# A mixture-of-experts stage whose indirect transfers each wait for an assigned tile of TensorE

## The chip, the core and the metric

The kernel runs on one core of one Trainium2 chip. The metric is the time of one execution on the device in microseconds; shorter is better. The kernel before takes 2303.66 us, the median of three runs that lie between 2303.51 and 2306.36 us.

The engines are named as the profile names them: PE (TensorE, matmuls; PEld is its weight load), DVE (VectorE), ACT (ScalarE), POOL (GpSimd), SP (SyncE, which only issues transfers here).

## The reference, cut to what matters

A batch of 16 sequences of 512 tokens with 128 features goes through two transformer layers. The change lies in the last stage, a mixture of experts that runs twice over all tokens:

```python
for _ in range(LOOPS):                     # 2
    z_norm = _rmsnorm(z, norm_w)
    scores = softmax(z_norm @ router_w)    # 8 experts
    topk_vals, topk_idx = top_k(scores, 2)
    ...                                    # weights of the two chosen, made to sum to 1
    mixed = sum over e of cw[:, e] * _swiglu(z_norm, w1[e], w3[e], w2[e])
    z = z + mixed
```

Each of the 8192 tokens needs only its two chosen experts. So the kernel sorts token rows by expert, runs matmuls on tiles of 128 rows that all belong to one expert, and brings the results back to the tokens.

## The kernel before, in words

`two_layers` runs the attention and feed-forward stages (`middle`, up to about 1500 us of the profile) and then `experts` (from line 1131 on), which the change touches.

**Groups, units, tiles.** A group is 8 blocks of 128 tokens; there are 8 groups, and two rounds (loops), so groups k = 0 to 15 are routed. The sorted rows are worked off in units: unit 0 holds group 0, units 1 to 7 two groups each, unit 8 one. A unit of one group has 23 tiles, one of two groups 39; in all N = 319 tiles, and `base_of` = 0, 23, 62, 101, 140, 179, 218, 257, 296 are the units' first tiles.

**One tile.** SP loads 128 sorted rows from `rows_in` (L1357), up to 8 tiles ahead, after waiting for `step_done` of the tile 7 before it; PE transposes them (L1407, one matmul instruction a tile, which makes it a good counter of tiles), multiplies by w1 and w3 of the expert (L1395), transposes the hidden rows (L1388) and multiplies by w2 (L1402), in a software pipeline that is 8 steps deep (LAG). ACT and DVE move and combine the results; ACT stores 128 rows to `rows_out` (L1465). PE raises the semaphore `step_done` by one at each step, up to N + LAG = 327.

**Side work.** Between the tiles the same engines do the routing of group k in 20 small stages (`side`), spread over 14 or 20 steps from `begin[k]` on. Groups 0 and 1 are done ahead of tile 0. The last stage, 19, writes the rows' addresses (`scat_idx`, L1695) and raises `scat_ready`. Stages 0 to 3 of a group k of 8 or more first add what the gather brought; their DVE instructions wait for that gather and sit in front of the tiles' own.

**Transfers of POOL.** POOL issues nothing here but indirect transfers of 128 rows of 512 bytes. A scatter `s<k>` (L1506) is 16 of them, tokens of group k to their sorted places; a gather `g<k>` (L1519) is 16 that bring the results of group k - 8 back. Each run of 16 is called a burst below. The order is written out by hand in `transfers`:

```python
transfers = ("s0 s1 s2 s3 g8 s4 s5 g9 s6 g10 s7 g11 s8 g12 s9 g13 s10 g14 s11 s12 g15 s13 g16 s14 g17 g18 s15 "
             "g19 g20 g21 g22 g23").split()
```

A scatter waits for the group's rows and for `scat_ready`. A gather waits until all tiles of its unit are stored, and from g11 on for the additions of the gather three before it, whose buffer it takes. Within a burst there are no waits. SP waits before a unit's first load for all scatters of that unit, so a late scatter holds the tile with which the unit begins.

Of the kernel before, what the change touches and what calls it, by code (L numbers as in the profile page):

```python
# [1170 lines left out]
def experts(nc, x, z, w, tri, ins, out, rows_in):  # L1171


    IT = 8
    GROUPS = BATCHES * TILES // IT
    CHUNKS = 4
    SIDES = (LOOPS + 1) * GROUPS
    RING, HELD = 8, 8
    TURN, MULT, LAG = 6, 2, 8
    BANKS = 3  # L1180
    STAGES = 20
# [4 lines left out]
    base_of = [sum(tiles_in[:u]) for u in range(UNITS + 1)]  # L1186
    N = base_of[UNITS]
# [6 lines left out]
    unit_of = [max(u for u in range(UNITS) if first_of[u] <= k) for k in range(LOOPS * GROUPS)]  # L1194
    EARLY = 2
    begin = {2: 0, 3: 14, 4: 29, 5: 47, 6: 63, 7: 78, 8: 95, 9: 115, 10: 135, 11: 157, 12: 179, 13: 201, 14: 223, 15: 246,
             16: 270, 17: 283, 18: 292, 19: 314, 20: 325}
    transfers = ("s0 s1 s2 s3 g8 s4 s5 g9 s6 g10 s7 g11 s8 g12 s9 g13 s10 g14 s11 s12 g15 s13 g16 s14 g17 g18 s15 "
                 "g19 g20 g21 g22 g23").split()

    def length(k):

        return 14 if k < GROUPS else 20 if k < LOOPS * GROUPS else 8
# [13 lines left out]
    def unit_at(n):  # L1217

        return max(u for u in range(UNITS) if base_of[u] <= n)

    def stored_by(u, s):

        return 16 * sum(1 for n in range(base_of[u + 1]) if n % RING == s)

    with ExitStack() as ctx:
        def sb(name, shape, dt):
            return ctx.enter_context(nc.sbuf_tensor("moe_" + name, shape, dt))

        def sem(name):
            return ctx.enter_context(nc.semaphore("moe_" + name))  # L1230
# [37 lines left out]
        lg, sh, sh2, pr, key, at = (  # L1268
            sb(name, [P, IT, EXPERTS], F32) for name in ("lg", "sh", "sh2", "pr", "key", "at"))
# [33 lines left out]
        step_done, x_copied = sem("step_done"), sem("x_copied")  # L1303
# [15 lines left out]
        def tiles_of(k):  # L1319

            return IT * (k % GROUPS)
# [20 lines left out]
        @block.sync  # L1342
        def _(sp):
            sp.dma_start(w13[:, :, 0:FF], ins["L1_ffn_w1"].rearrange("e d f -> d e f")).then_inc(w_in, 16)
            sp.dma_start(w13[:, :, FF:2 * FF], ins["L1_ffn_w3"].rearrange("e d f -> d e f")).then_inc(w_in, 16)
            for e in range(EXPERTS):
                sp.dma_start(w2[:, e, :, :], ins["L1_ffn_w2"][e].rearrange("(c f) d -> f c d", f=P)).then_inc(w_in, 16)
            for n in range(N):
                u = unit_at(n)
                if n == base_of[u]:  # L1350
                    sp.wait_ge(tables, u + 1)
                    for k in range(first_of[u], first_of[u] + sizes[u]):
                        sp.wait_ge(scattered[k % 3], 16 * 2 * IT * (k // 3 + 1))
                row = sp.value_load(row_of[0:1, n:n + 1], min_val=0, max_val=EXPERTS * CAP - P)
                if n >= RING:
                    sp.wait_ge(step_done, n - RING + 1)
                sp.dma_start(xin[:, n % RING, :], rows_in[u % CHUNKS][bass.ds(row, P), :]).then_inc(x_loaded[n % RING], 16)  # L1357
# [131 lines left out]
        @block.gpsimd  # L1489
        def _(pool):  # L1490
            pool.iota(iota_i[:, :], [[1, MOST]], base=0, channel_multiplier=0)
            pool.iota(reg_i[:, :], [[CAP, EXPERTS]], base=0, channel_multiplier=0)
            pool.iota(fall_i[:, :], [[-1, EXPERTS]], base=EXPERTS, channel_multiplier=0)
            pool.memset(upper[:, :], 1.0)
            pool.memset(ones[:, :], 1.0).then_inc(const, 1)
            pool.wait_ge(const, 1)
            pool.affine_select(out=upper[:, :], in_=upper[:, :], compare_op=ALU.is_gt, fill=0.0, base=0,
                               pattern=[[1, P]], channel_multiplier=-1).then_inc(const, 1)

            def scatter(k):  # L1500
                loop, t0, u = k // GROUPS, tiles_of(k), unit_of[k]
                pool.wait_ge(xn_ready, k + 1)
                pool.wait_ge(scat_ready, k + 1)
                for a in range(2):
                    for t in range(IT):
                        pool.indirect_dma_start(rows_in[u % CHUNKS],  # L1506
                                                bass.IndirectOffsetOnAxis(ap=scat_idx[:, loop, a, t0 + t:t0 + t + 1], axis=0),
                                                xn[:, k % 3, t, :], None).then_inc(scattered[k % 3], 16)

            def gather(k):  # L1510
                loop, t0, u = k // GROUPS - 1, tiles_of(k), unit_of[k - GROUPS]
                pool.wait_ge(tables, u + 1)
                for s in range(RING):
                    pool.wait_ge(y_stored[s], stored_by(u, s))
                if k >= GROUPS + 3:
                    pool.wait_ge(added, k - GROUPS - 2)
                for a in range(2):
                    for t in range(IT):
                        pool.indirect_dma_start(yg[:, k % 3, a, t, :], None, rows_out[u],  # L1519
                                                bass.IndirectOffsetOnAxis(ap=gat_idx[:, loop, a, t0 + t:t0 + t + 1], axis=0))\  # L1520
                            .then_inc(gathered[k % 3], 16)

            for name in transfers:
                if name[0] == "s":
                    scatter(int(name[1:]))
                else:
                    gather(int(name[1:]))

        @block.vector
        def _(dve):  # L1530
# [221 lines left out]
def two_layers(nc, ins, out):  # L1752
    with ExitStack() as ctx:
# [57 lines left out]

        z = sb("z", [P, BATCHES * TILES, DIM], F32)
        experts(nc, x, z, w, tri, ins, out.rearrange(rows, p=P), rows_in)


# [22 lines left out]
```

## Time and profile before

| | before |
|---|---|
| median of the timed runs | 2303.66 us (2303.51 to 2306.36) |
| the profiled execution, its span | 2763.4 us |
| up to the experts stage, in the profile | about 1500 us, then about 100 us without tiles |
| first and last tile transposed | 1599.98 us and 2701.29 us |
| PE, DVE, ACT, POOL busy, share of the span | 76%, 67%, 53%, 44% |
| mean granted TensorE clock | 0.886 of full speed |

The execution that was profiled has a span of 2763.4 us; it is 460 us, or 20%, longer than the median of the timed ones. The page gives no time for it beside the span. A busy time is that of one engine; its share is taken over stages with different limits, so it has to be read stage by stage. "Issue" and "remote" are names for a wait whose end the trace doesn't explain by an instruction of this core's engines.

### The profile page before, as it was taken

The page shows a single profiled execution, that of the slowest core. Times are in us where ns is not written, and L with a number is a line of the kernel's source. Part 1 is how long each engine was busy: PE and PEld are TensorE (multiplying, and loading weights), DVE is VectorE, ACT ScalarE, POOL GpSimd, SP SyncE. Part 2 cuts the span into 40 slices and gives each one's busy share as a digit, 9 for nine tenths or more (in the row PEclk, how much of TensorE's full clock was granted, in tenths as well). Part 3 has the DMA queues.
Part 4 walks back from the last instruction along what each step waited for, and adds up shares of the span by engine and source line. Part 5 has one row for each costly group of instructions (what it writes and reads, how often), then busy time and mean ns, then how long its engine had stood idle before and what let it go on. Part 6 is the DMA issues. An engine that isn't in the chain of part 4 may idle for free. (4 is left out here: it accounts for less than half of the span.)

```text
span 2763.4 us, 47500 instructions
## 1 busy us (share of the span) xinstructions
PE 2109.4 (76%) x14679; PEld 1039.5 (38%) x14679; DVE 1847.5 (67%) x5421; ACT 1458.9 (53%) x3354; POOL 1221.4 (44%) x1710
## 2 busy tenths in 40 slices
PE   5999999999899899999999464665747585556662
PEld 1222222222256444444444243443535353344441
DVE  8999999999767788888888453544434344344324
ACT  1888888888833477777777222332314232233231
POOL 5433434332102577777775344244443524443434
PEclk9999999999999899999999677887859677777876
DMA  6535444354101133333332122221212222222322
GB/s 161 138 99 142 116 124 131 101 147 116 40 1 46 48 94 94 89 76 72 94 94 49 57 61 65 60 69 59 76 56 74 67 66 64 65 68 62 88 75 82
DMA packets 224611, 226.95 MB, mean 82 GB/s; under 512 B 34032, under 2 KB 187504, under 8 KB 224368
## 3 DMA queue, kind: packets, MB, share of 16 engines
q1 hardware_dynamic: 152432, 164.62, 22.4%
q0 software_dynamic: 16384, 33.59, 4.1%
q10 hardware_dynamic: 55552, 25.71, 3.2%
q8 instruction: 127, 2.08, 0.3%
q14 instruction: 116, 0.95, 0.1%
HBM read 96.48 MB, written 125.76 MB: 80 GB/s over the span
## 5 line engine op out<-in xcount | busy, mean ns | idle before, releaser
L702 ACT ACTIVATE mid_PT<-mid_ps 128x512 f32<-128x512 f32 (+2 forms) x1792 | 913.6, 568 | 257.7 <-PE mid_ps L583 249.8
L785 DVE TENSOR_REDUCE mid_nmax<-mid_ps 128x1 f32<-128x512 f32 (+2 forms) x1280 | 776.2, 657 | 61.8 <-PE mid_ps L562 36.7
L562 PE MATMUL mid_ps<-KT,QT 48*128 48x512 bf16 (+3 forms) x2048 | 604.6, 351 | 68.3 <-DVE mid_nmax L785 49.7
L1395 PE MATMUL moe_ps<-moe_w,moe_xinT 128*128 x638 | 393.0, 702 | 315.6 <-issue 171.2
L583 PE MATMUL mid_ps<-QT,KT 64*128 64x512 bf16 (+3 forms) x2048 | 562.0, 346 | 2.6 <-ACT mid_PT L702 2.2
L1547 DVE TENSOR_TENSOR moe_h<-moe_ps,moe_sg 128x256 f32<-128x256 f32 x319 | 134.7, 422 | 518.4 <-ACT moe_sg L1459 279.9
L599 PE MATMUL mid_ps<-mid_PT,vv 128*32 128x512 f32 (+3 forms) x4096 | 464.5, 526 | 15.8 <-POOL mid_PT L914 12.0
L1450 ACT ACTIVATE moe_xinT<-moe_ps,norm_w 128x128 f32<-128x128 f32 x319 | 116.8, 366 | 677.4 <-remote 318.3
L1506 POOL DMA_INDIRECT rows_in<-moe_xn,moe_scat_idx x256 | 246.7, 964 | 462.0 <-DVE moe_scat_idx L1695 388.0
L562 PEld LDWEIGHTS mid_ps<-KT,QT 48*128 48x128 bf16 x2048 | 158.9, 94 | 585.5 <-DVE mid_nmax L785 397.6
L1519 POOL DMA_INDIRECT moe_yg<-rows_out,moe_gat_idx x256 | 245.1, 957 | 249.1 <-issue 122.1
L782 DVE CUSTOM_DVE_ANT_0 mid_PT<-mid_ps,mask 128x512 bf16<-128x512 f32 (+1 forms) x512 | 304.3, 619 | 68.6 <-PE mid_ps L562 63.7
L1402 PEld LDWEIGHTS moe_ps<-moe_w,moe_hT 128*128 128x128 f32 x1276 | 221.2, 217 | 198.1 <-issue 198.1
L1395 PEld LDWEIGHTS moe_ps<-moe_w,moe_xinT 128*128 128x128 f32 x638 | 112.5, 221 | 330.8 <-issue 330.4
L1402 PE MATMUL moe_ps<-moe_w,moe_hT 128*128 x1276 | 220.0, 301 | 12.5 <-issue 6.6
L914 POOL TENSOR_SCALAR_AFFINE_SELECT mid_PT<-mid_PT 128x512 f32<-128x512 f32 x256 | 154.8, 635 | 143.7 <-ACT mid_PT L702 142.3
L1388 PE MATMUL moe_ps<-ident,moe_h 128*128 128x128 f32 x638 | 139.6, 304 | 57.9 <-DVE moe_y L1556 41.5
L898 POOL TENSOR_TENSOR x<-x,mid_ao 128x256 f32<-128x256 f32 x32 | 23.2, 725 | 308.4 <-DVE mid_ao L801 308.4
L583 PEld LDWEIGHTS mid_ps<-QT,KT 64*128 64x128 bf16 x2048 | 136.0, 94 | 18.6 <-ACT mid_PT L702 14.9
L599 PEld LDWEIGHTS mid_ps<-mid_PT,vv 128*32 128x32 f32 x4096 | 81.5, 108 | 131.9 <-issue 96.0
L1454 ACT ACTIVATE moe_hT<-moe_ps 128x256 f32<-128x256 f32 x319 | 120.6, 378 | 15.5 <-remote 14.5
L1459 ACT ACTIVATE moe_sg<-moe_ps 128x256 f32<-128x256 f32 x319 | 123.7, 388 | 0.2
(265 smaller groups left out, 3025.7 us busy)
## 6 DMA issues: line engine op xcount, KB each, us to landing
l_spread<-mid_slots SPq DMA_DIRECT2D x128, 384.0 KB, 5.5
rows_in<-mid_blank SPq DMA_DIRECT2D x64, 512.0 KB, 4.3
QT<-l_spread SPq DMA_DIRECT2D x128, 192.0 KB, 4.3
KT<-l_spread SPq DMA_DIRECT2D x128, 192.0 KB, 5.2
moe_xin<-rows_in SPq DMA_DIRECT2D x319, 64.0 KB
rows_out<-moe_y ACTq DMA_DIRECT2D x319, 64.0 KB
x<-in_L_attn_x_dram SPq DMA_DIRECT2D x8, 512.0 KB, 6.6
QT<-mid_mrows SPq DMA_DIRECT2D x256, 6.0 KB
```

The lines of the kernel that those rows point to most:

```text
L562: mm = pe.matmul(ps[:, bank, n_keys * a:n_keys * (a + 1)], QT[rows, par, pair, i * P:(i + 1) * P], KT[rows, par, pair, 0:n_keys], start=Tr ...
L583: mm = pe.matmul(ps[:, bank, m * a:m * (a + 1)], KT[rows, own, pair, i * P:(i + 1) * P], QT[rows, own, pair, SEQ - m:SEQ], start=True, sto ...
L599: mm = pe.matmul(ps[32 * j:32 * j + 32, O, first(kt):SEQ], vv[:, ((r - 3) // 4) % 2, kt, 4 * ((r - 3) % 4) + j, :], weights_of(r - 3, kt, ...
L702: act.activation(weights_of(r, i, heads), ps[:, ring(S2, n - 2, k), 0:widths[i] * len(heads)], ACT.Exp, scale=scale).then_inc(exp_done, 1)
L782: dve.tensor_tensor_reduce(thrown[:, (SLOTS * n + k) % len(S1), 0:width(i)], of, w["mask"][:, SEQ - width(i):SEQ], -1.0, 3.0e38, ALU.add, ...
L785: dve.tensor_reduce(to, of, X_AXIS, ALU.max, negate=True).then_inc(s1_used, 1)
L914: pool.affine_select(out=diagonal, in_=diagonal, compare_op=ALU.is_ge, fill=0.0, base=0, pattern=[[0, 4], [1, P]], channel_multiplier=-1). ...
L1388: mm = pe.transpose(ps[:, bank, H + c * P:H + (c + 1) * P], h[:, v % 4, c * P:(c + 1) * P], w["ident"][:, :])
L1395: mm = pe.matmul(ps[:, GU[v % BANKS], :], xinT[:, v % 2, :], w13[:, bass.ds(expert(v), 1), :].rearrange("p a f -> p (a f)"), start=True, s ...
L1402: mm = pe.matmul(ps[:, bank, Y:Y + DIM], hT[:, v % 2, c * P:(c + 1) * P], w2[:, bass.ds(e, 1), c, :].rearrange("p a d -> p (a d)"), start= ...
L1506: pool.indirect_dma_start(rows_in[u % CHUNKS], bass.IndirectOffsetOnAxis(ap=scat_idx[:, loop, a, t0 + t:t0 + t + 1], axis=0), xn[:, k % 3, ...
L1519: pool.indirect_dma_start(yg[:, k % 3, a, t, :], None, rows_out[u], bass.IndirectOffsetOnAxis(ap=gat_idx[:, loop, a, t0 + t:t0 + t + 1], a ...
```

## The change

A new function `assigned` makes a list of 512 step numbers, one for each indirect transfer in the order of `transfers`. It starts from the step at which the burst can be ready (`ready`), lets the numbers grow by at least a half from transfer to transfer, so that no more than two have the same one, and then walks back so that no number is above that of the step at which the rows are needed (`due_at`). Before each indirect transfer POOL then waits until `step_done` has reached its number; numbers of zero or below give no wait. Nothing is removed or reordered; the waits ahead of a burst stay.

```diff
+    def assigned():
+
+        ready, due_at = [], []
+        for name in transfers:
+            k = int(name[1:])
+            if name[0] == "s":
+                ready += [0 if k < EARLY else begin[k] + 19 * length(k) // STAGES + 1] * (2 * IT)
+                due_at += [base_of[unit_of[k]] - RING] * (2 * IT)
+            else:
+                ready += [base_of[unit_of[k - GROUPS] + 1] + LAG + 1] * (2 * IT)
+                due_at += [begin.get(k, N + LAG + 1) - 1] * (2 * IT)
+        at, spread = -1.0, []
+        for r in ready:
+            at = max(r, at + 0.5)
+            spread.append(int(at))
+        latest = N + LAG
+        for i in range(len(spread) - 1, -1, -1):
+            latest = min(latest, due_at[i])
+            spread[i] = min(spread[i], latest)
+        return spread
...
+            def after_tile(tiles):
+
+                at = next(tiles)
+                if at > 0:
+                    pool.wait_ge(step_done, at)
...
                 for a in range(2):
                     for t in range(IT):
+                        after_tile(tiles)
                         pool.indirect_dma_start(rows_in[u % CHUNKS],
...
+            tiles = iter(assigned())
```

The same `after_tile(tiles)` stands before the indirect transfer of `gather`. Worked out, the list begins so: s0 gets no wait (its numbers are -8), s1 gets 8, 8, 9, 9 up to 15, 15, s2 gets 15 sixteen times, s3 28 to 35, g8 36 to 43, s4 44 to 51, s5 61 to 68, g9 71 to 78, s6 79 to 86, g10 87 to 94; and it ends with g21 305 to 312, g22 313 to 320 and g23 327 sixteen times.

## Rows read from the trace of the kernel before

**Rows 1.** Page: the span.

```profile
span 2763.4 us, 47500 instructions
```

**Rows 2.** Windows: length; busy us by engine (instructions), granted clock, DMA share, GB/s.

```profile
100.00:1400.00 1300.00, 1200.40 (x9652) 468.72 (x9650) 1134.69 (x2656) 968.10 (x1997) 592.42 (x972) 0.99 0.35 91
...
1600.00:1700.00 100.00, 69.58 (x332) 45.58 (x328) 60.83 (x284) 36.05 (x101) 39.31 (x41) 0.84 0.22 67
1700.00:2700.00 1000.00, 615.93 (x2953) 425.49 (x2954) 402.57 (x1705) 306.31 (x927) 404.67 (x423) 0.77 0.23 67
```

**Rows 3.** Windows of L1407 (one a tile; PE, then PEld): all, burst g13, undisturbed.

```profile
1700.00:2700.00 1000.00, 84.55 (x284) 44.92 (x284) 0.77 0.23 67
2129.50:2149.50 20.00, 1.09 (x4) 0.57 (x4) 0.76 0.28 74
2342.00:2370.00 28.00, 4.09 (x15) 2.15 (x15) 1.00 0.24 68
```

**Rows 4.** Timeline, PE, in the burst g13: start, length, instruction [idle before <-releaser].

```profile
2128.23 0.27 PE L1407 MATMUL moe_ps<-ident,moe_xin 128*128 128x128 f32 x1
...
2129.87 0.27 PE L1407 MATMUL moe_ps<-ident,moe_xin 128*128 128x128 f32 x1
...
2135.74 0.27 PE L1407 MATMUL moe_ps<-ident,moe_xin 128*128 128x128 f32 x1
...
2148.53 2.07 PE L1395 MATMUL moe_ps<-moe_w,moe_xinT 128*128 x2 [12.30 <-issue]
```

**Rows 5.** Waits, whole span: engine, line, what ended them: us, times, longest.

```profile
ACT moe_xinT L1450 <- remote: 318.3, 35, 22.9
```

**Rows 6.** Source lines of scatter (L1506) and gather (L1519): duration ns min/median/max.

```profile
L1506 POOL DMA_INDIRECT rows_in<-moe_xn,moe_scat_idx x256: 952/958/1202, 1573.2 to 2567.9; - x128
...
L1519 POOL DMA_INDIRECT moe_yg<-rows_out,moe_gat_idx x256: 938/944/1939, 1709.0 to 2751.5; - x128
```

**Rows 7.** Timeline, POOL: first and last of s1, first of s2.

```profile
1604.58 0.96 POOL L1506 DMA_INDIRECT rows_in<-moe_xn,moe_scat_idx  x1 [11.18 <-DVE moe_scat_idx L1695]
...
1623.51 0.96 POOL L1506 DMA_INDIRECT rows_in<-moe_xn,moe_scat_idx  x1 [0.30 <-issue]
1643.25 0.96 POOL L1506 DMA_INDIRECT rows_in<-moe_xn,moe_scat_idx  x1 [18.78 <-DVE moe_scat_idx L1695]
```

**Rows 8.** Timeline, POOL: last of s3, then first of g8.

```profile
1707.70 0.96 POOL L1506 DMA_INDIRECT rows_in<-moe_xn,moe_scat_idx  x1 [0.31 <-issue]
1708.96 0.98 POOL L1519 DMA_INDIRECT moe_yg<-rows_out,moe_gat_idx  x1 [0.30 <-issue]
```

**Rows 9.** Windows, all instructions: inside s1 with DVE at work, inside g13 with DVE idle.

```profile
1605.00:1610.00 5.00, 1.94 (x6) 0.58 (x4) 4.52 (x25) 1.54 (x6) 3.78 (x5) 1.00 0.30 90
2140.00:2144.00 4.00, 0.00 (x0) 0.00 (x0) 0.00 (x0) 0.00 (x0) 3.09 (x4) 0.50 0.21 58
```

**Rows 10.** Timeline, POOL, inside g13.

```profile
2142.00 0.94 POOL L1519 DMA_INDIRECT moe_yg<-rows_out,moe_gat_idx  x1 [0.30 <-issue]
2143.24 0.94 POOL L1519 DMA_INDIRECT moe_yg<-rows_out,moe_gat_idx  x1 [0.30 <-issue]
```

**Rows 11.** Timeline, PE and DVE, around s1: tiles' transposes, a chain of small DVE steps.

```profile
1615.90 0.27 PE L1407 MATMUL moe_ps<-ident,moe_xin 128*128 128x128 f32 x1
...
1624.93 0.42 PE L1407 MATMUL moe_ps<-ident,moe_xin 128*128 128x128 f32 x1
...
1603.62 0.17 DVE L1695 CAST moe_scat_idx<-moe_keep_at 128x16 int32<-128x16 f32 x1
...
1615.34 0.17 DVE L92 SCALAR_TENSOR_TENSOR moe_rstd<-moe_rtmp,moe_rstd 128x8 f32<-128x8 f32 x1 [1.22 <-DVE moe_rtmp L91]
```

**Rows 12.** Source L1516 of POOL: waits that stand as instructions of their own.

```profile
L1516 POOLq EVENT_SEMAPHORE  x13: 43/43/43, 1986.3 to 2729.9; - x13
```

**Rows 13.** Timeline, end: POOL's last transfer, DVE after it.

```profile
2751.54 0.94 POOL L1519 DMA_INDIRECT moe_yg<-rows_out,moe_gat_idx  x1 [0.30 <-issue]
2754.09 4.42 DVE L1568 SCALAR_TENSOR_TENSOR z<-moe_yg,moe_keep_w,z 128x128 f32<-128x128 f32 x16 [12.41 <-DMA moe_yg<-rows_out,moe_gat_idx]
```

More of the change, by code:

```diff
@@ L1498, in _, with scatter @@
                                pattern=[[1, P]], channel_multiplier=-1).then_inc(const, 1)
-            def scatter(k):
+            def after_tile(tiles):
+                at = next(tiles)
+                if at > 0:
+                    pool.wait_ge(step_done, at)
+            def scatter(k, tiles):
                 loop, t0, u = k // GROUPS, tiles_of(k), unit_of[k]
@@ L1508, in scatter, with gather @@
                                                 xn[:, k % 3, t, :], None).then_inc(scattered[k % 3], 16)
-            def gather(k):
+            def gather(k, tiles):
                 loop, t0, u = k // GROUPS - 1, tiles_of(k), unit_of[k - GROUPS]
@@ L1518, in gather @@
                     for t in range(IT):
+                        after_tile(tiles)
                         pool.indirect_dma_start(yg[:, k % 3, a, t, :], None, rows_out[u],
@@ L1521, in gather @@
                             .then_inc(gathered[k % 3], 16)
+            tiles = iter(assigned())
             for name in transfers:
                 if name[0] == "s":
-                    scatter(int(name[1:]))
+                    scatter(int(name[1:]), tiles)
                 else:
-                    gather(int(name[1:]))
+                    gather(int(name[1:]), tiles)
         @block.vector
```

## The prediction, made before the change was run

> **What bounds the kernel now.** I read the page's span first, then the windows by stretch, then a counter of tiles, then one burst of POOL in order of time.
>
> The span of the profiled execution is 2763.4 us [rows 1], 459.7 us above the median of 2303.66. This gap has to be placed before anything else, since the change works on the stretch in which it may lie. The windows tell the two halves apart [rows 2]: in the attention stages PE is busy for 1200 of 1300 us at a granted clock of 0.99, so there is little there to lose; in the experts stage it is busy for 616 of 1000 us at 0.77. The transpose that runs once a tile says how fast tiles go [rows 3]: 284 in those 1000 us, 3.52 us each, but 15 in 28 us (1.87 us each) in a stretch without indirect transfers, and only 4 in the 20 us of the burst g13. Read in order of time, g13 shows how [rows 4]: tiles come 1.64 us apart, go on for some 6 us of the burst, and then PE stands still for 12.3 us, until the burst is all but over. ACT's part of it is a wait "for remote" of 318.3 us in 35 pieces [rows 5]. During s1 even a DVE step that waits only for the DVE step before it sits idle for 1.22 us [rows 11], so it is no lack of rows: signals between and within engines come late while POOL issues.
>
> Are these stalls there in the timed runs? From 1700 to 2700 us they cost (3.52 - 1.87) x 284 = 469 us; in the 100 us before, 34 tiles ran, 100 - 34 x 1.87 = 36 us more, some of it honest waiting. Taking both away gives 2763.4 - 505 = 2258 us; the median is 2304. So the timed runs have room for about 45 us of all such stalls, a tenth of what the profile shows. I conclude, from this subtraction alone, that most of the stall belongs to the execution under the profiler.
>
> Without the stalls two queues are close to each other. PE: 319 tiles x 1.87 = 597 us from 1600 on, so the last tile at about 2197. POOL: one transfer takes 0.95 us [rows 6], but s1's first and last of 16 are 18.93 us apart [rows 7], 1.26 us each, 20.2 us a burst. The 31 bursts from s1 on take 626 us; from 1604.6 that is 2231 without a break. Walking the order by hand with tiles of 1.87 us, POOL has to wait for an index for about 9 us before s2 and 16 us before s3, and for 3 us in all at s5, s12 and s13; then from s7 on it mostly runs behind, by 10 to 50 us. That gives 2259 for the end of the last issue. In the profile the end comes 11.9 us after the last issue starts, so 10.6 after that transfer's 1.26 us [rows 1, 13]: 2270 us. The median is 34 us above this; that rest is unexplained, and is the most that smoother transfers could win. **POOL's queue, behind PE's in time but not in length, sets the end.**
>
> **The change, part by part.** It adds 496 waits (s0 has none) and removes nothing; all of them sit in POOL's queue, and behind each are only POOL's later transfers, no transfer of SP or ACT.
>
> *A wait that is already met.* The nearest row is a handover between bursts: g8 has nine waits of its own before its first transfer, all met, and that transfer starts 1.26 us after s3's last, with the same 0.30 us idle as inside a burst [rows 8]. So a met wait costs 0 us. The upper end is a wait that stands as an instruction and isn't covered, 0.043 us [rows 12]: 496 x 0.043 = 21 us on POOL. Below zero there is no reason: a met wait does nothing. I take 0, as this row is the same instruction on the same queue.
>
> *Which waits are met.* Two transfers a tile means one per 0.94 us at 1.87 us a tile; POOL needs 1.26. Sixteen transfers are spread over 8 tiles, 15 us, while POOL takes 20.2 us, nearly 11 tiles. So within a burst POOL falls behind its numbers, and the numbers bite only where a tile takes more than 2 x 1.26 = 2.52 us. At the start of a burst the number is that of the step after which its index or its stores exist at all, so it is met too; and where bursts follow each other, 8 tiles of number stand against 11 tiles of work. The last ones, g22 (up to 320) and g23 (327), wait for additions and for the last stores, which come later than those steps. Cost 0, covered by POOL's own slowness; if POOL were faster than 0.94 us a transfer, the burst would last 15 us instead, still less than now.
>
> *The exception is s1.* Its rows exist before tile 0, so its numbers have no such base; they follow s0's and begin at 8. Now it starts at 1604.58, 0.8 us after its index [rows 7, 11]. With the change it waits for the eighth step, tile 7, whose transpose starts at 1615.90 and takes 0.27 [rows 11]; plus the same 0.8 us it starts at 1617.0, 12.4 us later, and ends at 1637.2 instead of 1624.8. Its last number, 15, is met before. Behind it is s2, and behind s2 the first load of unit 1, tile 23. PE, not stalled, would be there about 28 us after tile 8, near 1650; s2's rows land after 1654 now, so PE waits there, and every us of s2 is one of the end. In the profile s2 starts at 1643.25 for want of its index [rows 7], 18.3 us after tile 8 at 1624.93 [rows 11]. Undisturbed, tile 8 comes about 4.5 us after tile 7 rather than 9.0 (half of it is the slow chain of DVE), at 1620.4; of the 18.3 us I take 4 off as stall, which puts s2 at 1635 now. Bounds: 1631 (8 us off), and 1639 (nothing off). So s2 moves to 1637.2 by 0 to 6 us, and 2 at 1635. Since POOL's later bursts leave little slack to catch up, I carry it whole, and take the middle of the bounds, +3.
>
> *A rule that speaks against the spread.* The row first: with DVE at work for 4.52 of 5 us, s1's transfers come every 1.26 us; in g13 with DVE idle, every 1.24 [rows 9, 10]. That is 0.02 us, or 10 us over 496 transfers if all moved from idle to busy DVE. The Trainium skill (SBUF — State Buffer, "SBUF: two separate sides") says that GpSimd can't write descriptors while DVE holds the port that they share, as some fp32 copies do; by it, transfers among live tiles should be much slower than in a stall. The trace doesn't agree here.
>
> **Sum** against the profiled execution: +3 us for s1, and less stall, since there tiles do take over 2.52 us in bursts and the waits bite. POOL then holds until tiles have moved on, and a burst needs at least 7 steps where g13 saw 4 tiles. If every burst ran at 2.5 to 3.3 us a tile (two transfers, without and with 0.8 us to restart), its 8 tiles would lose 5 to 11 us, 31 bursts 155 to 345, where 505 are lost now: a span of about 2410 to 2610 instead of 2763.4. The timed runs don't have this loss to give back: 2303.7 + 3 = **2306.7 us**.
>
> **The rivals.**
> *Faster: the timed runs stall too.* For it: DVE, ACT and PE stand still in nearly every burst, and the subtraction leaves 34 to 45 us. Against: stalls of 1 us a burst wouldn't bring tiles to 2.52 us, from where the waits bite. Half of 34 us gives 2303.7 - 17 + 3 = 2290; all of it 2273. Chance 0.24.
> *Slower: s1's delay passes whole.* One mechanism at one place: s2's index is ready before 1632.6, so that over 4.6 us pass to tile 23 and from there along POOL's full queue to the end. With the index at 1631, +6; at 1629, +8: 2312. For it: POOL's order leaves little slack. Against: s2's own index was late in the trace by 18.8 us after s1. Chance 0.18.
> *Slower: met waits cost something,* 0.043 us each on the queue that sets the end: 2306.7 + 21 = 2328; or 0.02 each, 2317. The handover row speaks against it. Chance 0.10.
> *It doesn't do what it says:* that two a tile is no limit at POOL's pace is my forecast itself; if s1's delay is hidden too, 2303.7, inside the forecast.
>
> **How the numbers follow.** About 0.2%, 4.6 us, is what a measurement of this kernel can tell from no change. Forecast (2303.7 to 2308, likeliest 2306.7): 0.48, all of it within 0.2%. Faster 0.24; slower 0.18 + 0.10 = 0.28. For 8 in 10, I leave out the deepest part of the faster case and the dearest of the waits: 2278 to 2316.
>
> **What would show it.** In the changed kernel's profile: s1's first transfer right after the eighth transpose, about 12 us later than before, and s2 directly behind it with 0.30 us idle; bursts longer than 20.2 us with 7 or more tiles in them; fewer "remote" waits of ACT; a higher granted clock; a span 150 to 350 us shorter, with the timed runs hardly moved. Wrong would be: timed runs that gain by over 5 us (the stalls are real), transfers more than 1.27 us apart where their step has long passed (a met wait costs), or s2 starting later for its index than for s1.

## The result, and the profile after

The changed kernel takes 2315.07 us (2312.49 to 2316.00, 7 runs) where the kernel before, on the same chip, takes 2306.36 us (2303.51 to 2309.72, 7 runs). The ratio is 1.0035, 95% interval 1.0025 to 1.0046: **slower by 8.7 us**. The time lies in the range, 1 us below its upper end, and the direction is that of the forecast, but the size is three times the forecast's +3, and the case that came true is the rival of s1's delay. Ratios here and below are of undisturbed executions; a single one was left out, of the kernel before beside the run e6, which took 10203 us.

The page after, span, engines and granted clock:

```profile
span 2312.2 us, 47503 instructions
...
PE 2014.7 (87%) x14679; PEld 984.0 (43%) x14679; DVE 1848.9 (80%) x5421; ACT 1460.8 (63%) x3354; POOL 1225.3 (53%) x1710
...
PEclk9999999999999998899999999976999999999996
```

The span is 2312.2 us, not some 2500, and the granted clock in the experts stage is mostly at 9 tenths or full. That can't be compared with the profile of before shown ahead of the prediction, for a reason that the experiments brought out and without which no number here can be read: **the chips that these runs fell on are of two kinds.** On three of those in the experiments the unchanged kernel before takes 2306 to 2308 us, on two 2760 to 2768 us, timed or profiled alike. The first profile of before, with its span of 2763.4 us, fits only the second kind, the timed runs beside it only the first. I call them *free* and *holding* chips. Each of the five was used for one set of runs, so whether the chip or its state at that time makes the kind isn't told apart. On a free chip the profile of before (the run e5 below) is this:

```profile
span 2304.9 us, 47500 instructions
...
PE 2010.8 (87%) x14679; PEld 982.8 (43%) x14679; DVE 1849.2 (80%) x5421; ACT 1462.2 (63%) x3354; POOL 1228.2 (53%) x1710
...
PEclk9999999999999999899999999985999999999996
```

So on equal ground the spans are 2304.9 and 2312.2 us, 7.3 apart, with PE's busy time 4 us more. How tiles go after the change: windows of L1428, the transpose that was L1407, in the burst g13 and over 500 us (PE busy, PEld busy, clock, DMA share, GB/s):

```profile
1929.60:1949.60 20.00, 2.06 (x7) 1.09 (x7) 0.86 0.38 104
1700.00:2200.00 500.00, 67.26 (x243) 35.35 (x243) 0.95 0.40 115
```

7 tiles in the 20 us of g13, where [rows 3] had 4; but before on a free chip has 7 in that burst too (e5), and both have 243 in the 500 us. Nothing was cured there, as nothing was ill.

Where the 7 us are: the start of the stage. After the change, POOL from s1 to s2, the index of s2 (DVE), and the transposes of tiles 22 to 25:

```profile
1614.88 0.95 POOL L1534 DMA_INDIRECT rows_in<-moe_xn,moe_scat_idx  x1 [18.48 <-PE moe_ps L1428]
...
1617.72 0.96 POOL L1534 DMA_INDIRECT rows_in<-moe_xn,moe_scat_idx  x1 [0.63 <-PE moe_ps L1428]
...
1634.19 0.96 POOL L1534 DMA_INDIRECT rows_in<-moe_xn,moe_scat_idx  x1 [0.30 <-issue]
1635.45 0.96 POOL L1534 DMA_INDIRECT rows_in<-moe_xn,moe_scat_idx  x1 [0.30 <-issue]
...
1630.13 0.17 DVE L1725 CAST moe_scat_idx<-moe_keep_at 128x16 int32<-128x16 f32 x1
...
1653.69 0.27 PE L1428 MATMUL moe_ps<-ident,moe_xin 128*128 128x128 f32 x1
...
1659.46 0.33 PE L1428 MATMUL moe_ps<-ident,moe_xin 128*128 128x128 f32 x1 [3.97 <-DMA moe_xin<-rows_in]
...
1662.91 0.42 PE L1428 MATMUL moe_ps<-ident,moe_xin 128*128 128x128 f32 x1
...
1665.06 0.27 PE L1428 MATMUL moe_ps<-ident,moe_xin 128*128 128x128 f32 x1
```

And before, on a free chip (e5), the firsts of s1 and s2 and the same four tiles:

```profile
1602.91 0.96 POOL L1506 DMA_INDIRECT rows_in<-moe_xn,moe_scat_idx  x1 [7.47 <-DVE moe_scat_idx L1695]
...
1630.09 0.96 POOL L1506 DMA_INDIRECT rows_in<-moe_xn,moe_scat_idx  x1 [7.21 <-DVE moe_scat_idx L1695]
...
1652.89 0.27 PE L1407 MATMUL moe_ps<-ident,moe_xin 128*128 128x128 f32 x1
...
1654.53 0.27 PE L1407 MATMUL moe_ps<-ident,moe_xin 128*128 128x128 f32 x1
...
1656.28 0.27 PE L1407 MATMUL moe_ps<-ident,moe_xin 128*128 128x128 f32 x1
...
1657.91 0.27 PE L1407 MATMUL moe_ps<-ident,moe_xin 128*128 128x128 f32 x1
```

s1 starts 12.0 us later, behind the eighth transpose; its third transfer waits 0.63 us for the ninth. (After is itself 1.0 us later at tile 0, so the change's part is 11.0 us.) s2's index is there at 1630.3, and s2, which before starts for it at 1630.09, now follows s1's last transfer with 0.30 us idle at 1635.45. PE comes to tile 23 and waits 3.97 us for the row load behind s2. The two executions differ by 0.8 us at tile 22, by 4.9 at tile 23, and by 7.2 at tile 25.

### The profile page after: what moved, and what is told of

The parts are those of the page before. It is cut to its first block and busy times, and to the rows that moved or that the text cites. A ratio compares the mean times of both kernels' runs of the same rounds, so it can differ in the third digit from the quotient of the medians.

```text
span 2312.2 us, 47503 instructions
## 1 busy us (share of the span) xinstructions
PE 2014.7 (87%) x14679; PEld 984.0 (43%) x14679; DVE 1848.9 (80%) x5421; ACT 1460.8 (63%) x3354; POOL 1225.3 (53%) x1710
## 5 line engine op out<-in xcount | busy, mean ns | idle before, releaser
L1416 PE MATMUL moe_ps<-moe_w,moe_xinT 128*128 x638 | 341.7, 618 | 0.2 <-DVE moe_h L1577 0.2
L1423 PEld LDWEIGHTS moe_ps<-moe_w,moe_hT 128*128 128x128 f32 x1276 | 197.5, 196 | 157.0 <-issue 157.0
L1423 PE MATMUL moe_ps<-moe_w,moe_hT 128*128 x1276 | 198.4, 279 | 0.0
L1409 PE MATMUL moe_ps<-ident,moe_h 128*128 128x128 f32 x638 | 129.3, 286 | 59.1 <-DVE moe_y L1586 58.0
L855 POOL TENSOR_TENSOR mcols<-mid_nmax,nought 128x16 bf16<-128x16 f32 x128 | 28.3, 221 | 161.6 <-DVE mid_nmax L785 161.6
```

The lines of the kernel that those rows point to most:

```text
L1409: mm = pe.transpose(ps[:, bank, H + c * P:H + (c + 1) * P], h[:, v % 4, c * P:(c + 1) * P], w["ident"][:, :])
L1416: mm = pe.matmul(ps[:, GU[v % BANKS], :], xinT[:, v % 2, :], w13[:, bass.ds(expert(v), 1), :].rearrange("p a f -> p (a f)"), start=True, s ...
L1423: mm = pe.matmul(ps[:, bank, Y:Y + DIM], hT[:, v % 2, c * P:(c + 1) * P], w2[:, bass.ds(e, 1), c, :].rearrange("p a d -> p (a d)"), start= ...
```

## The experiments

Three questions: is s1 the whole of the loss, what does a met wait cost, and what holds the tiles. Each ratio is to the kernel before on the same chip. All profiles here are of single executions.

### The kernel before, unchanged (e0, holding chip; e5, free chip)

No edit.

> The kernel before, unchanged, profiled a second time. Theory (the stalls in the bursts belong to one profiled execution, not to the kernel): a span of 2295 to 2320 us, granted clock about 0.96, 15 tiles in 28 us in bursts as elsewhere. Rival (before's bursts hold the tiles whenever they are profiled, and the change cures that): a span of about 2760 us again, with 4 tiles in 20 us of a burst. Timed, both expect the ratio 1.000 with an interval of about 0.001.

2768.32 us against 2767.91, ratio 1.0006 (0.999 to 1.0023): the *timed* runs were slow too. The page's span and the burst g13:

```profile
span 2762.8 us, 47500 instructions
```

```profile
2130.90:2150.90 20.00, 1.09 (x4) 0.58 (x4) 0.72 0.29 76
```

Four tiles in 20 us again. My theory, that this belonged to one profiled execution, fell. The rival had the span and the tiles right, but neither of the two expected timed runs of 2768 us: the stalls don't come from profiling.

> The kernel before, unchanged, to have its profile from a chip on which it takes about 2306 us, if these runs fall on one. Expected there: s1 starts near 1604, s2 near 1631.6 for its index, tile 23 near 1656 without waiting for its load, 15 tiles in 28 us in bursts too, span about 2305 us. On a chip of the other kind: 2760 us once more.

It fell on a free chip: 2306.86 us, span 2304.9, as shown above, with s1 at 1602.91, s2 at 1630.09 and tile 23 at 1654.53. In the burst g13 it has 7 tiles in 20 us, not the 10 or 11 I expected: PE waits for DVE's tables for 5.4 us up to 1937.5, inside that burst, and the granted clock is 0.50 in the 4 us behind it. The changed kernel has the same.

### s1 without its waits (e1, holding chip; e4, free chip)

```diff
             spread[i] = min(spread[i], latest)
+        spread[2 * IT:4 * IT] = [0] * (2 * IT)
         return spread
```

> The changed kernel without s1's 16 waits, a second time, since the first time fell on a chip where the kernel before takes 2768 us. If this chip gives 2306 us for the kernel before: theory (s1's late start makes the 8.7 us) expects a ratio of 0.999 to 1.001; the rivals (later waits, or met waits) expect 1.003 to 1.004. If it gives 2760 us: 0.925 to 0.933, as before.

On a free chip 2307.92 us against 2307.60, ratio 1.0003 (0.9994 to 1.0012). POOL's first of s1 and of s2, and tile 23:

```profile
1604.19 0.96 POOL L1535 DMA_INDIRECT rows_in<-moe_xn,moe_scat_idx  x1 [7.51 <-DVE moe_scat_idx L1726]
...
1631.60 0.95 POOL L1535 DMA_INDIRECT rows_in<-moe_xn,moe_scat_idx  x1 [7.47 <-PE moe_ps L1429]
...
1656.02 0.27 PE L1429 MATMUL moe_ps<-ident,moe_xin 128*128 128x128 f32 x1
```

s2 starts at 1631.60. Its row names PE, since its own wait for step 15 is the one named, but tile 14, of the 15th step, was transposed at 1628.44, and DVE wrote the index later, at 1630.66: s2 starts for its index, and tile 23 has no wait in its row. With s1's 16 waits gone and the other 480 in place, the loss is gone. So the waits from s2 on cost at most 0.0012 x 2307.6 = 2.8 us (the interval's upper end), all 480 together, on a free chip.

> The changed kernel, but the 16 transfers of s1 get no wait; all other waits stay. Theory (the 8.7 us come from s1's late start, which pushes s2 and tile 23): s1 starts near 1604, s2 near 1631, ratio to before 1.000, at most 1.001. Rival A (waits inside later bursts, or their restart, cost the time): ratio stays at 1.003 to 1.004. Rival B (met waits cost): ratio about 1.003.

The first try fell on a holding chip, where it says something else: 2574.99 us against 2767.91, ratio **0.9314** (0.929 to 0.9338), which none of the three had expected.

### Waits on s1 alone (e2, holding chip; e6, free chip)

```diff
             spread[i] = min(spread[i], latest)
+        spread[4 * IT:] = [0] * len(spread[4 * IT:])
         return spread
```

> e2_only_s1 a second time: the kernel before with waits on s1's 16 transfers alone. On a chip where the kernel before takes 2306 us: theory (s1's late start is enough by itself) expects 1.003 to 1.004, that is 7 to 9 us, with s2 about 4 us later. If other waits have a part in it, less. On a chip of the other kind: 1.0006 again, since 4 us are within its noise.

On a free chip 2314.90 us against 2308.26, ratio 1.0029 (1.0020 to 1.0038). First of s1, and tile 23:

```profile
1613.84 0.96 POOL L1535 DMA_INDIRECT rows_in<-moe_xn,moe_scat_idx  x1 [18.50 <-PE moe_ps L1429]
...
1658.37 0.47 PE L1429 MATMUL moe_ps<-ident,moe_xin 128*128 128x128 f32 x1 [3.83 <-DMA moe_xin<-rows_in]
```

The same late s1, and PE waits 3.83 us at tile 23. Taking s1's waits away removes the loss, and putting only them in makes it: on free chips s1 is shown to be the cause of nearly all of the 8.7 us. The two intervals overlap, so whether anything is left over (8.7 against 6.6 us) can't be told. The traces say the same: from tile 0 to g23's first transfer it is 673.7 us before (e5), 679.9 after, 681.6 with s1's waits alone (e6) and 673.4 with all but s1's (e4).

> The kernel before with waits on s1 alone (8, 8, 9, 9 to 15, 15); the 480 transfers from s2 on wait for nothing new. Theory (s1's late start is the cause): ratio 1.003 to 1.004, s2 directly behind s1, tile 23 waits for its load by about 4 us. Rivals A and B (later waits): ratio 1.000.

On a holding chip: 1.0006 (0.9988 to 1.0025). There s1 starts at 1618.04 and its burst is stretched by its own waits, yet s2, directly behind it, starts at 1641.16; in [rows 7] it starts at 1643.25, for an index that is late itself. So the late s1 makes no later s2.

### What a met wait costs (e3, holding chip)

```diff
+        spread[2 * IT:4 * IT] = [0] * (2 * IT)
+        spread[4 * IT:] = [1] * len(spread[4 * IT:])
         return spread
```

> s1 has no wait and each of the 480 transfers from s2 on waits for step 1, which is long past. This prices a met wait alone. Theory (a met wait costs nothing on POOL): ratio 1.000, transfers 1.26 us apart. Rival B (0.02 to 0.043 us each on the queue that sets the end): 10 to 21 us, ratio 1.004 to 1.009, transfers 1.28 to 1.30 us apart.

2764.55 us against 2767.91, ratio 1.0000 (0.9982 to 1.0019), and POOL inside a burst:

```profile
2132.49 0.96 POOL L1550 DMA_INDIRECT moe_yg<-rows_out,moe_gat_idx  x1 [0.30 <-issue]
2133.75 0.95 POOL L1550 DMA_INDIRECT moe_yg<-rows_out,moe_gat_idx  x1 [0.31 <-issue]
```

Transfers 1.26 us apart with the same 0.30 us idle as [rows 7, 10], each with a wait before it. A met wait costs nothing on POOL. These rows, and e4 on a free chip, carry that; the ratio alone wouldn't, since on a holding chip POOL waits for an index by over 20 us ahead of many bursts.

### The changed kernel on a holding chip (g0)

No edit.

> The changed kernel, unchanged, on whichever chip these runs get. If the kernel before takes about 2768 us there (tiles held in POOL's bursts): with the kernel without s1's waits at 0.931, theory says 0.93 to 0.935 here, s1's late start adding at most 6 us. If the kernel before takes about 2306 us there: 1.0035 again.

2558.24 us against 2759.61, ratio **0.9266** (0.9246 to 0.9286), span 2555.4. The change that loses 0.35% on a free chip wins 7.3% on a holding one, a little more than the 0.93 to 0.935 expected. POOL in g13, tiles in that burst, and ACT's wait:

```profile
2045.26 0.94 POOL L1548 DMA_INDIRECT moe_yg<-rows_out,moe_gat_idx  x1 [0.30 <-issue]
2048.02 0.94 POOL L1548 DMA_INDIRECT moe_yg<-rows_out,moe_gat_idx  x1 [1.82 <-remote]
...
2054.26 0.94 POOL L1548 DMA_INDIRECT moe_yg<-rows_out,moe_gat_idx  x1 [0.30 <-issue]
2056.82 0.94 POOL L1548 DMA_INDIRECT moe_yg<-rows_out,moe_gat_idx  x1 [1.62 <-PE moe_ps L1428]
```

```profile
2036.40:2059.30 22.90, 2.47 (x8) 1.32 (x8) 0.85 0.31 85
```

```profile
ACT moe_xinT L1471 <- remote: 177.7, 35, 9.8
```

POOL gets eight transfers out at 1.25 us, then stands for 1.82 us (its row says "remote", but the only wait written there is for a step), and for 1.62 us six transfers later. Eight tiles pass in 22.9 us instead of four in 20, and the unexplained waits of ACT shrink from 318.3 us [rows 5] to 177.7. They don't vanish.

### A pause of POOL's own instead of waits for tiles (p1, p2, holding chip; p3, p5, free chips)

The kernel before, with a scratch write after each indirect transfer (p2 has two):

```diff
+            def pause():
+                for _ in range(1):
+                    if pads:
+                        pool.wait_ge(padded, len(pads))
+                    pool.memset(pad[:, 0:512], 0.0).then_inc(padded, 1)
+                    pads.append(0)
...
                         pool.indirect_dma_start(rows_in[u % CHUNKS],
...
+                        pause()
```

> The kernel before, no new waits on tiles, but after each of the 512 indirect transfers POOL writes a scratch tile (a memset of 128x512, about 0.5 us), so that transfers come some 1.8 us apart rather than 1.26, by a clock of POOL's own. Where the kernel before takes 2768 us: theory C (signals queue up behind POOL's transfers because these come faster than something drains, and a slower pace alone cures it) expects tiles no longer held, ratio 0.92 or less. Theory D (what helps is that POOL waits for a tile, not its pace) expects the tiles held as before for longer bursts, ratio above 1.03. Where the kernel before takes 2306 us: 512 x 0.5 = 260 us on POOL's queue, of which over 150 show at the end, ratio about 1.07 to 1.1.

2473.24 us against 2759.61, ratio **0.8951** (0.8929 to 0.8973). POOL in g13, and tiles in that burst:

```profile
2009.97 0.95 POOL L1529 DMA_INDIRECT moe_yg<-rows_out,moe_gat_idx  x1 [0.16 <-issue]
2010.93 0.54 POOL L1506 MEMSET moe_pad<- 128x512 f32 x1
2011.63 0.95 POOL L1529 DMA_INDIRECT moe_yg<-rows_out,moe_gat_idx  x1 [0.16 <-issue]
```

```profile
2006.50:2032.80 26.30, 3.82 (x14) 2.00 (x14) 1.00 0.38 101
```

Transfers 1.66 us apart, 14 tiles in 26.3 us, which is 1.88 us a tile at full clock, and no row of "remote" among the experts stage's waits. POOL knows nothing of tiles here, so theory D is out: tiles go free without a wait for them. The pace is the likely reason, but it isn't separated from what else the edit brings, the memset as such and POOL's wait for its own last memset.

> As p1_pause with two such memsets, transfers about 2.3 us apart. Where the kernel before takes 2768 us: theory C expects no held tiles at all, and the time set by POOL's queue, 512 x 2.3 = 1180 us from 1576 on, about 2780 us. Theory D expects held tiles on top, above 3000 us.

A single execution: 2769.41 us, close to the 2780 worked out. Here too no wait of ACT is "for remote", as theory C expects. The loss is now POOL's queue: SP waits 486.8 us for scatters before units' first loads.

```profile
SPq L1355 <- DMA rows_in<-moe_xn,moe_scat_idx: 486.8, 9, 77.5
```

> As p1_pause with a memset of half the size, 128x256 (about 0.3 us), transfers about 1.42 us apart instead of 1.66. Where the kernel before takes 2760 us: theory C with a drain faster than one transfer in 1.42 us expects free tiles and POOL's queue at the end shorter by 512 x 0.24 = 123 us at most, 2380 to 2420 us, ratio 0.865 to 0.88; with a drain between 1.42 and 1.66 us, tiles held again in the bursts' second halves, ratio 0.90 to 0.95. Theory D expects 0.99 to 1.03. Where the kernel before takes 2306 us: ratio 1.01 to 1.04.

It fell on a free chip: 2371.87 us against 2307.60, ratio 1.0282 (1.0266 to 1.0297). There is nothing to free there, and the pause costs, transfers being 1.46 us apart:

```profile
1901.35 0.97 POOL L1515 DMA_INDIRECT rows_in<-moe_xn,moe_scat_idx  x1 [0.17 <-issue]
...
1902.81 0.96 POOL L1515 DMA_INDIRECT rows_in<-moe_xn,moe_scat_idx  x1 [0.16 <-issue]
```

> p3_short_pause a second time, since it fell on a chip where the kernel before takes 2306 us. On a chip where that takes 2760 us: theory C with a drain faster than one transfer in 1.46 us expects free tiles, 2370 to 2420 us, ratio 0.86 to 0.88; with a drain between 1.46 and 1.66 us, tiles held in the second halves of bursts, ratio 0.90 to 0.95. On a chip of the first kind: 1.028 again.

A free chip again: 2370.65 against 2307.32, ratio 1.0276 (1.0259 to 1.0293). So whether 1.46 us would be slow enough on a holding chip stays open; if it is the pace, tiles begin to be held somewhere between 1.66 and 1.26 us a transfer.

The free-chip runs tell one thing more. The pause makes POOL's queue longer by about 496 x 0.20 = 99 us, but only 64 us show at the end. So the queue of the kernel before had some 35 us of slack (an estimate, from these two numbers).

**A version that beats both?** The changed kernel without s1's waits (e1, e4): like the kernel before on a free chip (1.0003), better than the changed kernel's 1.0035 there, and 0.9314 on a holding one. Against the changed kernel on a holding chip it wasn't run on the same chip (0.9314 and 0.9266 are from two), so which of the two is better there is open.

## Why the prediction was right and wrong, step by step

**Where the stalls belong: wrong, and lucky.** The step "most of the stall belongs to the execution under the profiler" compared a span with a median and named the profiler as the only difference. The chip differed too. e0's timed runs at 2768 us show it. The forecast survived by luck: the timed runs came from a free chip, which really had little to give back. Had the comparison run on a holding chip, the forecast would have missed by 200 us. Of the 8.4 us between 2306.7 and 2315.07, 2.7 are the kernel before itself (2306.36 over seven runs, not 2303.66 over three), the rest is s1's term.

**"POOL's queue sets the end": wrong on a free chip.** The chain of work that ended last, on the page of e5, covers the experts stage and runs over PE, with POOL in it for 2% of the span:

```profile
PE 18%; DVE 7%; ACT 3%; issue 2%; POOL 2%; DMA 0%; ACTq 0%; SPq 0%; POOLq 0%; DVEq 0%
```

From tile 0 to tile 318 at 2251.12 the chain is in the tiles; only from g22 at 2251.27 on is it in POOL. Ahead of s5, s12 and s13 POOL waits 13.48, 13.47 and 6.81 us for an index that the tiles' side work writes, 33.8 us where the walk had 3:

```profile
1740.75 0.96 POOL L1506 DMA_INDIRECT rows_in<-moe_xn,moe_scat_idx  x1 [13.48 <-DVE moe_scat_idx L1695]
```

Those 31 us are nearly all of the 34 us that the prediction left unexplained, and agree with the slack of some 35 us that the pause showed. The walk went wrong by its pace of tiles, as follows.

**The 34 to 45 us left over: a term was missing.** I took 1.87 us for every tile. On a free chip (e5) PE's first and last transposes are 651.5 us apart, 2.04 us a tile, and this is what the window that I picked didn't hold:

```profile
1630.77 0.27 PE L1407 MATMUL moe_ps<-ident,moe_xin 128*128 128x128 f32 x1
1637.38 0.69 PE L1388 MATMUL moe_ps<-ident,moe_h 128*128 128x128 f32 x2 [6.33 <-DVE moe_y L1556]
...
1640.42 0.42 PE L1407 MATMUL moe_ps<-ident,moe_xin 128*128 128x128 f32 x1
```

```profile
PE moe_ps L1388 <- DVE moe_y L1556: 58.8, 36, 6.3
```

After tile 16 PE waits 6.33 us for DVE, which builds a unit's tables (L1709 to L1742) ahead of the tiles' own copies, and resumes with matmuls of nearly double the length. Such waits are 58.8 us in 36 pieces, eight of them 4.0 to 6.3 us long, one for the tables of each unit but the first. They are about the 54 us by which the last tile comes later than forecast (2251, not 2197), and the faster rival's 34 us weren't there to win.

**A met wait costs 0: right.** e3 and e4. The handover row was the right neighbour.

**Which waits are met: right on free chips,** where bursts after s1 last 20.0 to 21.4 us but for g22 (22.0), as in e5. On a holding chip they bite as worked out, at 2.9 us a tile, inside the 2.5 to 3.3 given; the span of 2555.4 lies within 2410 to 2610.

**s1's start: right in place, mis-sized twice.** s1 moves by 11.0 to 12.0 us in the traces (12.4 forecast). The first error is the time of s2 before the change: I got 1635; undisturbed it is 1630.1, below my own lower bound of 1631. The 4 us that I took off the 18.3 behind tile 8 were right: on a free chip it is 13.9 us from tile 8 to s2. But I had put tile 8 at 1620.4, and it is at 1616.20, since stalls lay ahead of it too: tile 7 comes 3.1 us earlier (1612.82, not 1615.90) and tile 8 3.4 us behind it, not 4.5. So s2 moved by 5.4 us in the traces, 4.4 counted from tile 0, not 2. The second error is "carried whole": a delay of 4 us at tile 23 doesn't stay 4. The rows of the wait at tile 23 say so, windows of after, then of before on a free chip at the same tiles (the columns of [rows 2]; before's row begins right after its tile 25):

```profile
1655.00:1659.00 4.00, 0.49 (x5) 0.30 (x3) 1.60 (x8) 0.00 (x0) 0.60 (x1) 1.00 0.17 51
1659.00:1663.00 4.00, 3.25 (x10) 1.97 (x11) 0.62 (x2) 0.91 (x3) 0.00 (x0) 0.69 0.24 68
1663.00:1667.00 4.00, 4.00 (x29) 2.97 (x27) 1.02 (x5) 3.59 (x9) 0.00 (x0) 0.88 0.31 86
```

```profile
1658.00:1662.00 4.00, 3.61 (x28) 2.40 (x27) 2.24 (x11) 3.96 (x10) 0.00 (x0) 1.00 0.28 78
```

PE is busy 0.49 of 4 us, then the granted clock is 0.69 in the next 4 us and 0.88 in the following, the lower of its two levels for part of each; before, it is 1.00 from 1650 to 1666, around tiles 22 to 29. The 3.97 us of waiting became 6.4 us by tile 25 (7.2 less the 0.8 that the executions differed by at tile 22), and the end keeps it: g23's last transfer starts 7.3 us later. The rival, priced at +6 with the index at 1631, was right up to tile 23. Behind it the factor of 1.6 was missing, and the delay went along the tiles on PE, not "along POOL's full queue": by s11, before the wait ahead of s12, POOL was only 5.7 us later than in e5, while the tiles of that time were 7.2 us later.

**Transfers beside a busy DVE: right for most DVE instructions, wrong for one.** I compared transfers in two stretches [rows 9, 10] and found no difference. The same trace of e5 has eight additions of x and z, of 1.22 us each, and seven of them run beside transfers. The transfer that starts during one takes 1.19 to 1.98 us, where 0.95 is usual:

```profile
2172.58 1.22 DVE L1610 TENSOR_TENSOR x<-x,z 128x1024 f32<-128x1024 f32 x1
...
2172.65 1.98 POOL L1506 DMA_INDIRECT rows_in<-moe_xn,moe_scat_idx  x1 [0.30 <-DVE z L1568]
```

The seven add 4.6 us in all, and the longest bursts (s15, g22) have them. After the change the same seven add 4.9 us, so they have no real part in the 8.7 us. The Trainium skill (SBUF — State Buffer, "SBUF: two separate sides") says that GpSimd waits for the whole of a DVE instruction that holds the port they share, one in a 2-port mode or, against a GpSimd instruction that reads SBUF, one with two SBUF inputs. The trace agrees with it for this instruction, and it was too much to say that it doesn't agree. That the port is the cause wasn't tested.

## What to carry to other kernels

Before a difference between a profile and the timed runs is put down to the profiler, time and profile the same kernel on the same chip: here one unchanged kernel took 2306 or 2768 us by chip, and the change was worth +0.35% or -7.3%. Two queues that are close in length have to be told apart by the waits in them: here POOL's had 31 us of waits more than the walk gave it, and the tiles set the end. A wait that paces a queue must not reach transfers that something else needs soon: 16 of 496 waits made nearly all of the loss. Their clip ("no later than the step at which the rows are needed") gave s1 and s2 the same last step, 15, and left no room for the 20 us that s2 takes behind s1 in the same queue. And a short idle of PE is priced with the slow matmuls after it, here 4 us of waiting as 6.4.

## What the runs showed of the hardware that I had not expected

- Two kinds of chips: 2306 to 2308 us on three chips of the experiments, 2768 and 2760 us on two, with no difference on POOL: transfers are 1.25 to 1.26 us apart on both. Each chip was used once, so a state that passes isn't excluded.
- On holding chips, a few transfers into a burst, PE, ACT and DVE stand still at once (PE for 12.3 us in [rows 4]), and even DVE's step behind its own step waits 1.22 us [rows 11]. With transfers 1.66 us apart and a memset between them it is gone. What fills up, and why on some chips only, is open: no run told signals that come late from instructions that come late, or a queue from a slower path.
- On free chips DVE's tables, some 7 us of work once a unit, cost PE 4.0 to 6.3 us of idle each time, and the granted clock is 0.50 to 0.62 in the 4 us behind it.
- A DVE addition of 128x1024 beside an indirect transfer goes with a transfer of up to 1.98 us instead of 0.95.
